# Attention's inverse row sums through a DRAM table, and one weight split moved between engines

## The reference

```python
x = x + _L0_xattn_ref(_layernorm(x, axis=-1), ctx_2048, ctx_2048, gamma)
x = x + _L0_ffn_ref(_layernorm(x, axis=-1), router_w, w_gate, w_up, w_down, sw_gate, sw_up, sw_down, shared_gate_w)

# _L0_xattn_ref(q, k, v, gamma), B=4, 512 channels = 8 heads of dq=dv=64, Lq=Lk=512
qk = jnp.einsum('bhdq,bhdl->bhql', qh, kh) * scale
sm = jax.nn.softmax(qk, axis=-1)
ret = jnp.einsum('bhql,bhdl->bhdq', sm, vh)
return gamma * ret.reshape(B, Dv, Lq)

# _L0_ffn_ref: 2048 rows of 512, 8 experts of inner size 352, two per row, a shared expert of 1408
shared = jnp.einsum('ts,sh->th', silu(x @ sw_gate) * (x @ sw_up), sw_down)
h = silu(jnp.einsum('th,ehi->eti', x, w_gate)) * jnp.einsum('th,ehi->eti', x, w_up)
routed = jnp.einsum('eth,te->th', jnp.einsum('eti,eih->eth', h, w_down), combine)
return routed + sigmoid(x @ shared_gate_w)[:, None] * shared
```

## Time and profile before

| | us |
|---|---|
| median of 3 runs (lowest, highest) | 878.79 (876.71, 879.09) |
| the profiled execution | 879.82 |
| its span | 878.1 |
| busy in the span: PE | 849.9 |
| DVE, ACT, POOL | 566.7, 503.4, 447.3 |

### The profile page before, as it was taken

One profiled execution on the slowest core, in us unless ns is written; L12 is line 12 of the kernel. 1 busy time (PEld: TensorE's weight loads), 2 busy tenths in 40 slices (PEclk: granted clock), 3 DMA queues, 4 the chain that ended last, 5 costly groups with the idle time before them and its releaser, 6 DMA issues.

```text
span 878.1 us, 13766 instructions
## 1 busy us (share of the span) xinstructions
PE 849.9 (97%) x4624; PEld 708.6 (81%) x4624; DVE 566.7 (65%) x820; ACT 503.4 (57%) x861; POOL 447.3 (51%) x430
## 2 busy tenths in 40 slices
PE   6999999999999999999999999999999999999993
PEld 3677777777788888888888888888899999999992
DVE  6999999999656414321212121118899999999991
ACT  4899999999653211211111111116788888888881
POOL 5576888875700000144330000003899999999974
PEclk9999999999999999999999999999999999999997
DMA  3124442321453382001320023547744443443442
GB/s 96 61 91 138 133 143 97 132 84 61 156 161 93 85 49 96 1 2 33 112 26 1 0 97 106 191 159 265 216 84 77 85 80 72 81 86 72 76 69 36
DMA packets 63237, 81.24 MB, mean 93 GB/s; under 512 B 15370, under 2 KB 34826, under 8 KB 63187
## 3 DMA queue, kind: packets, MB, share of 16 engines
q1 hardware_dynamic: 53426, 60.14, 22.7%
q0 software_dynamic: 9760, 20.49, 13.1%
HBM read 53.01 MB, written 27.60 MB: 92 GB/s over the span
## 4 chain that ended last, share of the span: by engine, by line
PE 92%; POOL 2%; issue 1%; DMA 1%; DVE 1%; ACT 1%; POOLq 0%; ACTq 0%; DVEq 0%
PE scores L1450 9%; PE scores L1451 9%; PE scores L1452 9%; PE scores L1311 7%; PE bank L1320 6%; PE bank L1464 5%; PE bank L1465 5%; PE bank L1466 5%; PE bank L1334 4%; PE bank L1336 3%; PE bank L1564 3%; PE bank L1565 3%; PE bank L1566 3%; PE bank L1533 3%; PE bank L1535 3%; PE bank L1534 3%
## 5 line engine op out<-in xcount | busy, mean ns | idle before, releaser
L1091 DVE TENSOR_TENSOR sg<-scores,sg 128x512 f32<-128x512 f32 x44 | 30.4, 692 | 201.3 <-PE scores L1452 201.2
L1450 PE MATMUL scores<-x_hl,wsp 128*128 128x512 f32 x352 | 137.2, 390 | 0.0
L1452 PE MATMUL scores<-x_hl,wsp 128*128 128x512 f32 x352 | 137.0, 389 | 0.0
L1451 PE MATMUL scores<-x_hl,wsp 128*128 128x512 f32 x352 | 137.0, 389 | 0.0
L644 POOL DMA_INDIRECT slot_rows<-msrc,posi x32 | 36.1, 1129 | 170.7 <-PE scores L1452 164.3
L659 POOL DMA_INDIRECT xg<-x_normed_rows,meta x39 | 38.5, 988 | 160.0 <-PE scores L1474 141.6
L815 ACT ACTIVATE sg<-scores 128x512 f32<-128x512 f32 x44 | 26.3, 598 | 158.4 <-PE scores L1452 158.4
L822 ACT ACTIVATE hh<-sg 128x512 fp32r<-128x512 f32 x44 | 27.8, 632 | 115.0 <-DVE sg L1091 100.0
L999 DVE TENSOR_TENSOR ptl<-bank,pth 128x512 fp32r<-128x512 f32 x128 | 87.3, 684 | 8.6 <-ACT pth L727 8.1
L721 ACT ACTIVATE pb<-scores,negmax 128x512 f32<-128x512 f32 x128 | 88.1, 694 | 4.6 <-DVE negmax L989 4.6
L727 ACT ACTIVATE pth<-bank 128x512 fp32r<-128x512 f32 x128 | 76.7, 600 | 12.3 <-PE bank L1320 11.1
(11 more groups left out here) (197 smaller groups left out, 2228.0 us busy)
## 6 DMA issues: line engine op xcount, KB each, us to landing
wex<-in_L_ffn_w_gate SPq DMA_DIRECT2D x8, 704.0 KB, 4.4
wex<-in_L_ffn_w_up SPq DMA_DIRECT2D x8, 704.0 KB, 5.8
xb<-in_x SPq DMA_DIRECT2D x16, 256.0 KB, 2.8
cn<-in_ctx SPq DMA_DIRECT2D x16, 256.0 KB, 2.8
x_rows<-xb SPq DMA_DIRECT2D x16, 256.0 KB, 2.0
x_normed_rows<-x2n SPq DMA_DIRECT2D x16, 256.0 KB, 2.0
x_normed_transposed<-x2T SPq DMA_DIRECT2D x16, 256.0 KB, 2.0
x_hl<-x_normed_transposed SPq DMA_DIRECT2D x4, 1024.0 KB, 5.3
```

Of the source, the lines that this page charges most:

```text
L1450: te.matmul(bk[:, :], hi, xhi, start=(h == 0), stop=False)
L1451: te.matmul(bk[:, :], hi, xlo, start=False, stop=False)
L1452: ins = te.matmul(bk[:, :], lo, xhi, start=False, stop=(h == HC - 1))
```

## The change

The inverse row sums no longer go through POOL's spreading, PE and ACT. POOL's `inverses` multiplies the 128x8 `rinv` by gamma into `rgs`. SP stores the two heads' columns of `rgs` into a small DRAM tensor `inv_d` (`store_inverses`, two DMAs of 512 separate 4-byte elements each), waits for these, and loads each head's row of 512 back, repeated over 64 partitions, into `rgam` (`load_inverses`, two DMAs of 64 rows of 2 KB each). PE's four transposes and ACT's copy per tile are gone, and so are the waits for them. In SP's `step(i)`, `load_inverses(i-1)` stands behind `load_values(i+2)`, and `store_inverses(i)` behind `load_x(i+4)`.

In the last slots, the third block of slot 37's down weights is split by ACT (`down_tail_hi`) and DVE (`down_tail_lo`), each right behind its split of the first two blocks. POOL's list there becomes `scatter(36)`, `down_tail(38)`, `scatter(37)`, `scatter(38)`.

```diff
@@ sync
+            def store_inverses(t):
+
+                sp.wait_ge(g_rgs, t + 1)
+                after(sp, g_att, t - 1)
+                for s in range(2):
+                    sp.dma_start(inv_d[t % 2, s, :].rearrange("(c p) -> p c", p=P), rgs[:, :, s], allow_slow_non_contiguous=True).then_inc(st_inv, 16)
+
+            def load_inverses(t):
+                sp.wait_ge(st_inv, 32 * (t + 1))
+                after(sp, g_att, t)
+                for s in range(2):
+                    sp.dma_start(rgam[DH * s:DH * (s + 1), :], inv_d[t % 2, s, :].partition_broadcast(DH)).then_inc(ld_inv, 16)
...
                 if there(i + 2):
                     load_values(i + 2)
+                if there(i - 1):
+                    load_inverses(i - 1)
                 if there(i - 3):
                     store_columns(i - 3)
                 if there(i + 4):
                     load_x(i + 4)
+                if there(i):
+                    store_inverses(i)
...
@@ gpsimd
-            def spread(t):
+            def inverses(t):
 
                 g.wait_ge(d_rinv, t + 1)
-                after(g, e_R, t)
-                gp.tensor_copy(rspr[:, :, :], rinv[:, :, :].rearrange("p c s -> p (c s)").unsqueeze(2).to_broadcast([P, 2 * QC, DH])).then_inc(g_rspr, 1)
+                after(g, st_inv, 32 * t)
+                if t == 0:
+                    g.wait_ge(ld_small, 48)
+                gp.tensor_scalar(rgs[:, :, :], rinv[:, :, :], gam[:, :], None, ALU.mult).then_inc(g_rgs, 1)
 
             def scaled(t):
 
                 g.wait_ge(d_att, 2 * t + 2)
-                g.wait_ge(a_Rg, t + 1)
+                g.wait_ge(ld_inv, 32 * (t + 1))
...
-                    if s == SLOTS - 3:
-                        scatter(s)
-                    if s + 1 < SLOTS:
+                    if s + 1 < SLOTS and s + 1 != SLOTS - 2:
                         down_tail(s + 1, experts[j])
-                    if s != SLOTS - 3:
-                        scatter(s)
+                    scatter(s)
@@ scalar
-            def inverses(t):
-
-                act.wait_ge(e_R, t + 1)
-                after(act, g_att, t)
-                sc.activation(rgam[:, :], bT[1][:, :], ACT.Copy, scale=gam[:, :]).then_inc(a_Rg, 1)
...
+            def down_tail_hi(e):
+                sc.activation(wd3[0:IR, 0, 2 * H:3 * H], wex[0:IR, e, 2 * W3 + 2 * H:EW], ACT.Copy).then_inc(a_wt, 1)
...
                     down_hi(s + 1, e1)
+                    if isinstance(s, int) and s == SLOTS - 3:
+                        down_tail_hi(e1)
@@ vector
+            def down_tail_lo(e):
+                dve.wait_ge(a_wt, 1)
+                ve.tensor_tensor(wd3[0:IR, 1, 2 * H:3 * H], wex[0:IR, e, 2 * W3 + 2 * H:EW],
+                                 wd3[0:IR, 0, 2 * H:3 * H].bitcast(F32), ALU.subtract).then_inc(d_wt, 1)
...
                     down_lo(s + 1, e1)
+                    if isinstance(s, int) and s == SLOTS - 3:
+                        down_tail_lo(e1)
@@ tensor
-                    freed((d_vl, 1, i, 0), (d_ptl, 8, i - 1, 1), (a_x2T, 1, i - 4, 0), (a_Rg, 1, i - 2, 0))
-                    inverses(i - 1)
                     times_v(i - 1, 1 - par, 3)
...
                     if c == IC - 1:
-                        pe.wait_ge(g_wd, s + 1)
+                        if isinstance(s, int) and s == SLOTS - 2:
+                            pe.wait_ge(d_wt, 1)
+                        elif isinstance(s, int) and s == SLOTS - 1:
+                            pe.wait_ge(g_wd, SLOTS - 1)
+                        else:
+                            pe.wait_ge(g_wd, s + 1)
```

More of the change, by code:

```diff
@@ L69, in xattn_moe_kernel @@
     xT_d = nc.dram_tensor("x2_normed_transposed", (NT, P, H), F32, kind="Internal").ap()
+    inv_d = nc.dram_tensor("inverse_sums", (2, 2, L), F32, kind="Internal").ap()
     meta_d = nc.dram_tensor("slot_rows", (SLOTS * P, 2), I32, kind="Internal").ap()
@@ L137, in xattn_moe_kernel @@
         att = [place(f"att{j}", [P, L]) for j in range(2)]
-        rspr = place("rspr", [P, 2 * QC, DH])
+        rgs = place("rgs", [P, QC, 2])
         rgam = place("rgam", [P, L])
@@ L239, in xattn_moe_kernel @@
         e_vt, a_vh, d_vl = sem("e_vt"), sem("a_vh"), sem("d_vl")
-        e_s, d_max, a_exp, d_rinv, g_rspr, e_R, a_Rg = sem("e_s"), sem("d_max"), sem("a_exp"), sem("d_rinv"), sem("g_rspr"), sem("e_R"), sem("a_Rg")
+        e_s, d_max, a_exp, d_rinv, g_rgs = sem("e_s"), sem("d_max"), sem("a_exp"), sem("d_rinv"), sem("g_rgs")
+        st_inv, ld_inv = sem("st_inv"), sem("ld_inv")
         e_t, a_pth, d_ptl, e_pv = sem("e_t"), sem("a_pth"), sem("d_ptl"), sem("e_pv")
@@ L259, in xattn_moe_kernel @@
         d_k0, a_q0 = sem("d_k0"), sem("a_q0")
+        a_wt, d_wt = sem("a_wt"), sem("d_wt")
         st_meta0, st_meta = sem("st_meta0"), sem("st_meta")
@@ L625, in step @@
                 if there(i):
-                    spread(i)
+                    inverses(i)
                 if there(i + 2):
@@ L683, in down_tail @@
                 gp.tensor_copy(w[0:IR, 0, c], wex[0:IR, e, 2 * W3 + (IC - 1) * H:EW]).then_inc(g_wh, 1)
-                g.wait_ge(g_wh, s + 1)
+                g.wait_ge(g_wh, s + 1 if s < SLOTS - 2 else SLOTS - 1)
                 gp.tensor_tensor(w[0:IR, 1, c], wex[0:IR, e, 2 * W3 + (IC - 1) * H:EW], w[0:IR, 0, c].bitcast(F32), ALU.subtract).then_inc(g_wd, 1)
@@ L993, in inverse @@
                 dve.wait_ge(a_exp, 8 * t + 8)
-                after(dve, g_rspr, t)
+                after(dve, g_rgs, t)
                 ve.reciprocal(rinv[:, :, :], rsum[:, :, :]).then_inc(d_rinv, 1)
@@ L1336, in times_v @@
                 te.matmul(bO[:, :], v, ptl[n % 4][:, :], start=False, stop=(c == LC - 1)).then_inc(e_pv, 1)
[L1338 to L1343, removed]
             def values_T(t, half, par):
@@ L1386, in step @@
                 if there(i - 3):
-                    freed((a_Rg, 1, i - 1, 0), (d_vl, 1, i, 0), (d_ptl, 8, i - 1, 1), (a_x2T, 1, i - 4, 0))
+                    freed((d_vl, 1, i, 0), (d_ptl, 8, i - 1, 1), (a_x2T, 1, i - 4, 0))
                     rows_T(i - 3, 1 - par)
@@ L1403, in step @@
                 if there(i):
-                    freed((a_x2T, 1, i - 3, 0), (a_Rg, 1, i - 1, 0), (d_vl, 1, i, 0), (d_ptl, 8, i - 1, 1))
+                    freed((a_x2T, 1, i - 3, 0), (d_vl, 1, i, 0), (d_ptl, 8, i - 1, 1))
                     probs_T(i, par, 1)
@@ L1416, in step @@
                 if there(i + 1):
-                    freed((d_ptl, 8, i, 1), (a_x2T, 1, i - 3, 0), (a_Rg, 1, i - 1, 0), (d_vl, 1, i, 0))
+                    freed((d_ptl, 8, i, 1), (a_x2T, 1, i - 3, 0), (d_vl, 1, i, 0))
                     values_T(i + 1, half + par, 1 - par)
@@ L1508, in _ @@
             gate_up(0, 0, 0)
-            pe.wait_ge(a_Rg, NT)
             rows_T(NT - 2, 0)
```

## The result

| | before | after |
|---|---|---|
| median, us | 877.89 (4 runs) | 889.40 (4 runs, 886.95 to 895.26) |
| profiled execution | 879.82 | 888.93 |
| its span | 878.1 | 887.2 |

The ratio is 1.0141, interval 1.0116 to 1.0167. The change costs some 12 us, where a gain of 8 was forecast.

The account below looks back on a forecast made before the run. PE, holding 92% of the chain of waits, was taken as the bound. Attention -6.3, its end +0.3 and last slots -1.8 gave -7.8: 872.0 us profiled, 871.0 timed, range 869.0 to 875.2.

Parts of the forecast that it names:

- Removed from attention: Attention: PE's four transposes leave the chain, 0.44 us in each of fifteen tiles, 6.6 us; 6.3 counted after small stalls.
- the tight handover at `values_T`: Attention, PE's `values_T` needing DVE's `ptl(1)`: holds if `ptl(1)` comes 0.2 us earlier per tile, which freed ACT time gives.
- The last slots: Last slots: PE's 1.91 us wait at `hidden_T(38)` goes and the last scatter comes earlier; gain 1.8 us, bounds 0 and 1.9.
- The table's trip: Attention, store and load of `rgs` through DRAM: 10 of 14.6 us, hidden; store taken as 4.5 us.
- The row with small pieces: Profile row used to scale the store: DRAM write of the slot table, 4992 pieces of 8 bytes, landing after 17.5 us.
- The load ... 2.8 us: Attention, loading the table into `rgam`: 256 KB in rows of 2 KB, priced like `xb<-in_x` at 2.8 us.
- SP's list ... Cost 0: Attention, SP's queue: four more issues per tile, at most 2 us of a queue that mostly waits; cost 0.
- End of attention, 0.3: Last tile: `rgam(15)` loads behind a 1 MB load and may hold `scaled(15)`; loss up to 1.4 us, 0.3 taken.
- Rival 3: POOL's `scaled(t)` in attention: the DRAM trip is late and the kernel slower, 886 at 1 us a tile; chance 0.07.
- The bound of 17.5 us for the store: Attention, the table's store: upper bound from the slot table's DRAM write; with the load, a tile loses 5.7 us.
- the window: Attention, from `rgs` ready to `scaled` of the same tile: 14.6 us in which store and load must finish.
- The rules from "DMA: Bandwidth & Descriptors": Attention, DRAM trip: one descriptor per element and two 2 us latencies plus pieces, some 8 us, also hidden.

## Why the prediction was wrong

- *Removed from attention, 6.6 us on the chain, 6.3 counted:* right. Without the table tiles are 13.17 us apart for 13.18, and the mark comes 6.6 us earlier. So the tight handover at `values_T` held.
- *The last slots, 1.8 us:* the chain behaves as worked out, and the traces show 0.8 to 3.5 us; the timed runs show 0.8 and can't tell it from nothing.
- *The table's trip, "Scaled by count, 1024 pieces take 3.6 us ... I take 4.5":* this step failed, and it turned the sign: with nothing but the store's pieces changed, the kernel takes 869.3 to 871.0. The row with small pieces wrote 8 bytes each; nothing in the trace before had written 4-byte neighbours. The store took 9.2 to 12.0 us for 4.5, a little over twice.
- *"The load ... 2.8 us", in the same step:* it landed after 2.8 to 7.3 us (median 3.2). The text had seen for the last tile alone that the load may stand behind a big one; it does in five tiles, and they hold 21.0 of POOL's 32.6 us. A store of 10 us and a median load of 3.2 come to 13.2 of 14.6 us; so little cover is left that what the load waits in the queue, and SP's list, decide. In ten of sixteen tiles POOL waited for the row.
- *"SP's list ... Cost 0":* SP waits for the store inside its one list, and the queue's other transfers slow down (2.0 to 7.2 us for `x_rows`). A late store delays `load_x` and all behind it, though no engine but DVE in the first tiles waited for `load_x`, as before. Above some 10.4 us (the estimate above) the store makes SP's round longer than a tile. The kernel in which POOL doesn't wait for the row lost 4.3 us by all this, with POOL's wait for the store in it.
- *End of attention, 0.3:* POOL waited 4.9 us for the row of the last tile. With 16-byte pieces it waited 1.0 to 1.3.
- *Rival 3* named place and kind rightly and had 0.07. Its threshold, a trip over 14.6 us, is where the kernel after stands. Its path was right in two places only: POOL's lateness reaches PE mostly through what stands behind `scaled` in POOL's list. Its price left out PE's clock. The bound of 17.5 us for the store stood in the text, above the threshold; with the window at less than three times the guess, that outcome deserved more weight than one in fourteen.
- *The rules from "DMA: Bandwidth & Descriptors"* of the Trainium skill (one descriptor per element, section "Rules for kernel authors"; 2 us fixed, section "Anatomy of one DMA — SWDGE (gpsimd) path", given there for DMAs that GpSimd issues, where these are SP's) gave an estimate of some 8 us for the trip, hidden as well, and no nearer: the store alone took 9.2 us or more. The count of descriptors doesn't order the stores measured here: 1024 pieces took 2.1 us or 10.

## What to carry to other kernels

A transfer's cost must be taken from one with the same piece size and the same spacing at its destination; a factor of two is nothing until it crosses the window that hides it, so work out the window and ask how likely the miss is. If a value must be turned through DRAM, choose which rows sit on which partition so that each partition writes a run of 8 bytes or more (3.7 us here; 1.8 with 16 bytes), and let the engine with slack do the reordering. An in-order list hands on lateness to everything behind the waiting instruction, related to it or not. And a kernel built so that nobody waits for a transfer must be checked for the waits that are left, such as the one that guards a buffer.

## What the runs showed of the hardware

- Stores to DRAM in 4-byte pieces without gaps took 8.8 to 17.1 us (two DMAs of 512 pieces, or one), and the same pieces 8 bytes apart 4.5, 32 bytes apart 2.5. 512 pieces of 8 bytes without gaps took 3.7. Why 4-byte neighbours cost so much no run shows; that stays open.
- While such a store is under way, other transfers of the same queue land late: 256 KB to DRAM in 7.2 us instead of 2.0; with the pieces 32 bytes apart it was 2.0 again.
- PE's weight load of 64x128 took 306 to 330 ns with a column step of four, 183 to 186 ns without; a transpose that writes PSUM with a step of four took 276 ns, as without.
- A POOL operation of 128x512 took 1.28 us with its write scattered over every 128th column, 0.77 with a plain one.
- After PE had waited 2.5 and 4.2 us in a full stage, its granted clock was 0.53 and 0.54 over the next 3.6 us.
